# Turning the row maxima of four attention heads with one transpose of eight columns in a two-layer kernel

## The chip, the cores and the metric

The kernel runs on one NeuronCore of one Trainium2 chip. The metric is the time of one execution on the device in microseconds (us), less is better. Five engines work side by side, each through its own list of instructions in a fixed order: TensorE (PE in the profile, with its weight loads as PEld), VectorE (DVE), ScalarE (ACT), GpSimd (POOL) and SyncE (SP), which here only issues the DMAs. They wait for one another through semaphores.

## The reference, cut to what matters

Input is `x` of 8 sequences x 256 positions x 128 features in float32. There are two layers. The part that the change touches is the attention of layer 0, of which there are two kinds:

```python
# kind B: a cell of six nodes, each an attention with 8 heads of 16 features
scores = einsum('bqhd,bkhd->bhqk', qh, kh) / sqrt(16)
attn   = softmax(scores)                      # over the 256 keys
ctx    = einsum('bhqk,bkhd->bqhd', attn, vh)
# kind A: an encoder block with 16 heads of 8 features
att = softmax(einsum('nqd,nkd->nqk', qm, km)) # plus a relative position bias
```

A softmax needs, for every query of every head, the largest score of the row, which is subtracted before the exponential. Layer 1 is a state space block (convolution, scan, gating, a feed-forward part) and a mixture of eight experts; its work fills the engines beside the attention.

## The kernel before, in words

One sequence after the other is computed, with the next sequence's layer 0 overlapping the present one's layer 1. The work is cut into stages such as `("max", "B", g)` or `("expert", 3)`, in four lanes: the cell (kind B), its side work, the encoder block (kind A) and layer 1. For every engine the tables `PLACES` and `START` give each stage a place in time; `order(engine)` sorts by it, and that is the order in which the engine goes through its stages. Nothing is reordered at run time, so a stage that waits holds all that stands behind it on its engine. The change touches none of these tables.

Heads go in groups of four, each head's features in a strip of 32 partitions. A sequence has 12 groups of kind B and 4 of kind A, so 16 groups, and the program has 128. A group goes through these steps:

- `maximum` (TensorE, L785): 16 matrix products give the scores of four heads with the queries on the partitions, 4 heads x 2 halves of 128 queries x 256 keys, in two wide PSUM tiles, `strips`.
- `tops` (VectorE, L1307): two reductions over the keys leave `rowmax`, 128 partitions x (4 heads x 2 query halves), so one column per head and half.
- `max_rows` on TensorE (L793): `rowmax` is turned, so that the maxima lie along the free dimension. Two transposes are made, one for each query half: each has four columns as the stationary operand (one per head, every second column of `rowmax`) and the 128 x 128 identity as the moving operand, and writes 4 partitions x 128 of a PSUM bank.
- `max_rows` on ScalarE (L1059): a copy of 4 x 256 values from PSUM to `maxrow` in SBUF.
- `max_rows` on SyncE (L601): a DMA of 4 KB puts the four rows as one more row into each head's strip of the query tile. The key tile has -1 there.
- `score` (TensorE, L802): waits for that DMA (`maxed`), then computes the scores again, now with the keys on the partitions and the maximum already subtracted.
- `exp` (ScalarE, L1066), and `values` (TensorE, L815 and L822) follow.

Small products share three PSUM banks in turn. `take` (L694) waits until the stage that had the bank three uses ago has been read; the rows of maxima are one such use, and ScalarE's copy sets its bank free. `maxrow` has two buffers for each side and kind, which a copy may overwrite after the DMA of two groups before has landed.

Of the kernel before, what the change touches and what calls it, by code (L numbers as in the profile page):

```python
# [12 lines left out]
ACT = mybir.ActivationFunctionType  # L13
AX = mybir.AxisListType.X

P = 128
NSEQ, L, D = 8, 256, 128
# [6 lines left out]
STRIP = 32  # L24
# [155 lines left out]
def hybrid_layers(nc, t):  # L180

    ctx = ExitStack()
    with ctx:
        def sb(name, shape, dt=F32):
            return ctx.enter_context(nc.sbuf_tensor(name, shape, dt))

        def one(name):
            return ctx.enter_context(nc.semaphore(name))

        def sig(name, per, step=1, sides=1):  # L190
            return Signal([one(f"{name}{i}" if sides > 1 else name) for i in range(sides)], per, step)

        def past(eng, s, b, k=0):
            if b >= 0:
                eng.wait_ge(*s.at(b, k))
# [6 lines left out]
        ident = sb("ident", [P, P])  # L202
# [4 lines left out]
        rows = sb("rows", [P, t["rows"].shape[0], D])  # L207
# [44 lines left out]

        sides = {"B": 2, "A": 1}
        rowmax = {k: sb(f"rowmax_{k}", [P, n, 2, 4, 2]) for k, n in sides.items()}
        maxrow = {k: [[sb(f"maxrow_{k}{j}{i}", [4, L]) for i in range(2)] for j in range(n)] for k, n in sides.items()}
        probs = sb("probs", [P, 2, 4, 2, L])
        out_sb = sb("out_sb", [P, 2, 512])
        rsum_b = sb("rsum_b", [P, 2, BH])
# [113 lines left out]
        maxrow_done = {"B": sig("maxrow_done_B", 2 * NODES, 1, 2), "A": sig("maxrow_done_A", A_GROUPS)}  # L372
# [65 lines left out]
        s_strips, s_valued, s_ps = one("strips_ready"), one("valued"), one("ps_ready")  # L438
# [51 lines left out]
        def ready(eng, b, name):  # L490
            eng.wait_ge(s_ps, PS_AT[b, name] + 1)
# [12 lines left out]
        def bank(b, name):  # L504
            return BANK[b, name]
# [12 lines left out]
        def _(sp):  # L518
# [20 lines left out]
            for i in range(2):  # L539
                dst = bass.AP(tensor=a_scr.tensor, offset=i * AH * STRIP * L, ap=[[L, P], [P * L, A_GROUPS], [1, L]])  # L540
# [55 lines left out]
            def max_rows(b, kind, k):  # L596
                sp.wait_ge(*maxrow_done[kind].at(b, k))
                side, row = (b % 2, BW) if kind == "B" else (0, AW)
                x = qs["B"][side][:, k % 2, :] if kind == "B" else qs["A"][:, k, :]
                dst = bass.AP(tensor=x.tensor, offset=x.offset + row * x.ap[0][0], ap=[[STRIP * x.ap[0][0], 4], [1, L]])  # L600
                sp.dma_start(dst, maxrow[kind][side][k % 2][:, :]).then_inc(maxed[kind][k % 2].of(b), 16)  # L601

            def o_write(b):
# [19 lines left out]
            def store(b):  # L623
                sp.wait_ge(*acc_done.at(b, EX))
                hold(sp, s_held)
                sp.dma_start(t["out"][b].rearrange("(a p) d -> p a d", p=P), acc[:, :, :]).then_inc(out_stored.of(b), 16)

            run_stages("sync", {"load": load, "a_write": a_write, "rows": max_rows, "t_rows": t_rows, "a_stack": a_stack, "pos": positions, "v_read": v_read_,
                                "o_write": o_write, "o_read": o_read_, "weights": weights, "store": store})
            sp.wait_ge(*out_stored.at(NSEQ - 1))  # L630
# [3 lines left out]
        def _(pe):  # L634
# [3 lines left out]
            n = 0  # L638
# [11 lines left out]
            for c in range(NODES):  # L650
                (eq, _), (ek, _), (ev, _) = PLAN[c]
                o = setup_banks[n % len(setup_banks)]
                setup([(o[:, 0:2 * P], raw_we_t[:, eq, :], raw_wq[:, c, :, :], True, True),
                       (o[:, 2 * P:4 * P], raw_we_t[:, ek, :], raw_wk[:, c, :, :], True, True)], len(setup_banks))
                o = setup_banks[n % len(setup_banks)]
# [8 lines left out]
            for c in range(NODES - 1):  # L664
                pe.wait_ge(s_dve0, 2 * NODES)
                o = ps[n % 2]
# [27 lines left out]
            def take(b, name):  # L694

                if FREED[b, name]:
                    user, freed, k = FREED[b, name]
                    pe.wait_ge(*freed.at(user, k))
                return bank(b, name)
# [88 lines left out]
            def max_rows(b, kind, k):  # L788
                pe.wait_ge(*top_done[kind].at(b, 2 * k + 1))
                o = take(b, ("rows", kind, k))  # L790
                side = b % 2 if kind == "B" else 0
                for qc in range(2):
                    mm = pe.transpose(o[0:4, qc * P:(qc + 1) * P], rowmax[kind][:, side, k % 2, :, qc], ident[:, :])  # L793
                mm.then_inc(s_ps, 1)

            def score(b, kind, g):
                pe.wait_ge(*maxed[kind][g % 2].at(b, g // 2))
# [169 lines left out]
            def expert(b, i):  # L967
# [5 lines left out]
                for j in range(2):  # L973
# [7 lines left out]
            run_stages("tensor",  # L981
                       {"prep_t": prep_t, "aproj": aproj, "q": queries, "k": keys, "v": values_in,
                        "values_a": values_a, "max": maximum, "rows": max_rows, "score": score, "values": values,
                        "post_b": lambda b, c: post(b, "B", c), "post_a": lambda b, g: post(b, "A", g),
                        "ctx": ctx_t, "node": node, "gather": gather, "wo_y": wo_y, "ab_t": ab_t_, "ff_y": ff_y,
# [5 lines left out]
        def _(act):  # L991
# [59 lines left out]
            def max_rows(b, kind, k):  # L1051
                ready(act, b, ("rows", kind, k))
                n, sides_n = (2 * NODES, 2) if kind == "B" else (A_GROUPS, 1)

                if k >= 2:
                    act.wait_ge(*maxed[kind][k % 2].at(b, k // 2 - 1))
                else:
                    past(act, maxed[kind][k % 2], b - sides_n, n // 2 - 1)
                act.activation(maxrow[kind][b % sides_n][k % 2][:, :], bank(b, ("rows", kind, k))[0:4, 0:L], ACT.Copy).then_inc(maxrow_done[kind].of(b), 1)  # L1059

            def exp(b, kind, g, i):
                strips_ready(act, b, "score", kind, g)
# [125 lines left out]
            def expert(b, i):  # L1188
                ready(act, b, ("h", i))
                if i >= 2:  # L1190
# [3 lines left out]
            run_stages("scalar",  # L1194
                       {"prep_t": prep_t, "aproj": aproj, "q": queries, "k": keys, "v": values_in, "values_a": values_a,
                        "rows": max_rows, "exp": exp, "out": out, "ctx": ctx_t, "node": node, "gather": gather, "ab_t": ab_t_,
                        "z_t": z_t, "inproj": inproj, "xc": xc_tanh, "bcdt": bcdt, "sp_u": sp_u_, "sp_z": sp_z, "state": state,
                        "h_t": h_t_, "ffn": ffn, "ffn_t": ffn_t, "router": router, "expert": expert})
# [541 lines left out]
```

## Time and profile before

| | |
|---|---|
| Median of three runs | 1611.76 us (1611.71 to 1615.91) |
| The profiled execution's own time | 1618.7 us |
| Its span, first to last instruction | 1616.9 us |
| TensorE busy | 1284.9 us, 79% of the span |
| VectorE busy | 1067.4 us, 66% |
| ScalarE busy | 743.6 us, 46% |
| GpSimd busy | 272.7 us, 17% |
| Mean granted clock of TensorE | 0.905 of 2.4 GHz |

The profile is one execution on the chip. The granted clock is what part of full speed TensorE was given; 1.00 is 2.4 GHz and 0.50 is 1.2 GHz. The chain of waits is followed back from the last instruction: at each step to the work that released it, or to the instruction before it on its engine; "issue" on it is time in which the engine waited for nothing that the profile shows. The duration of one matrix product goes from its start to its modelled end, and products overlap, so what a product costs in a stream of others is the distance to the next start, and not its duration.

### The profile page before, as it was taken

The page shows a single profiled execution, that of the slowest core. Times are in us where ns is not written, and L with a number is a line of the kernel's source. Part 1 is how long each engine was busy: PE and PEld are TensorE (multiplying, and loading weights), DVE is VectorE, ACT ScalarE, POOL GpSimd, SP SyncE. Part 2 cuts the span into 40 slices and gives each one's busy share as a digit, 9 for nine tenths or more (in the row PEclk, how much of TensorE's full clock was granted, in tenths as well). Part 3 has the DMA queues.
Part 4 walks back from the last instruction along what each step waited for, and adds up shares of the span by engine and source line. Part 5 has one row for each costly group of instructions (what it writes and reads, how often), then busy time and mean ns, then how long its engine had stood idle before and what let it go on. Part 6 is the DMA issues. An engine that isn't in the chain of part 4 may idle for free.

```text
span 1616.9 us, 28690 instructions
## 1 busy us (share of the span) xinstructions
PE 1284.9 (79%) x10896; PEld 888.4 (55%) x10896; DVE 1067.4 (66%) x1757; ACT 743.6 (46%) x1420; POOL 272.7 (17%) x277
## 2 busy tenths in 40 slices
PE   6767787778997799878987899779987898678328
PEld 5434454445784468545764577446754675347217
DVE  2322335486768866896779676886689667857775
ACT  0133344455555554555545555555455554443322
POOL 0000002022101311131103210221013110321260
PEclk9777998889998999899998999899989998789659
DMA  5042020001210122002100211012200210012102
GB/s 200 7 72 23 2 44 8 1 6 46 54 55 3 25 63 70 5 14 70 49 29 14 54 46 49 2 25 64 70 5 17 68 57 18 14 29 71 42 1 69
DMA packets 108359, 62.98 MB, mean 39 GB/s; under 512 B 71169, under 2 KB 90145, under 8 KB 108097
## 3 DMA queue, kind: packets, MB, share of 16 engines
q1 hardware_dynamic: 108224, 61.15, 14.0%
q8 instruction: 90, 1.47, 0.4%
q14 instruction: 45, 0.36, 0.1%
HBM read 54.02 MB, written 6.59 MB: 37 GB/s over the span
## 4 chain that ended last, share of the span: by engine, by line
PE 56%; DVE 22%; issue 10%; ACT 9%; DMA 2%; POOL 1%; SPq 0%; DVEq 0%; ACTq 0%; POOLq 0%
PE strips L802 10%; PE strips L785 7%; PE ps L963 6%; PE ps L975 6%; PE attn_out L815 6%; DVE rowmax_B L1307 5%; ACT probs L1066 5%; DVE hb L1448 5%; DVE hb L1443 3%; PE ps L742 2%; PE attn_out L822 2%; DVE rowmax_A L1307 2%; PE ps L646 2%; DVE work L1417 2%; PE ps L793 1%
## 5 line engine op out<-in xcount | busy, mean ns | idle before, releaser
L1066 ACT ACTIVATE probs<-strips 128x1024 f32<-128x1024 f32 x256 | 248.9, 1021 | 133.0 <-PE strips L802 132.3
L1307 DVE TENSOR_REDUCE rowmax_B<-strips 128x4 f32<-128x1024 f32 x192 | 227.1, 1218 | 119.6 <-PE strips L785 119.5
L802 PE MATMUL strips<-qs_b,ks_b 32*128 32x256 f32 x1536 | 129.6, 457 | 75.3 <-ACT probs L1066 45.8
L1448 DVE TENSOR_TENSOR_SCAN hb<-da,hb 128x1024 f32<-128x1024 f32 x64 | 150.2, 2346 | 2.2
L1534 DVE SCALAR_TENSOR_TENSOR work<-hb,ps 128x512 f32<-128x512 f32 x128 | 86.5, 686 | 96.7 <-ACT hb L1192 96.2
L802 PEld LDWEIGHTS strips<-qs_b,ks_b 32*128 32x128 f32 x1536 | 83.3, 213 | 106.4 <-issue 103.4
L785 PE MATMUL strips<-ks_b,qs_b 32*128 32x256 f32 x1536 | 114.2, 412 | 23.1 <-ACT probs L1066 12.4
L975 PE MATMUL ps<-ze,w_e 128*128 128x256 f32 x512 | 127.3, 386 | 3.2 <-DVE work L1534 1.8
L963 PE MATMUL ps<-w_e,work 128*128 128x128 f32 x1024 | 125.1, 277 | 1.2 <-DVE work L1534 1.2
L963 PEld LDWEIGHTS ps<-w_e,work 128*128 128x128 f32 x1024 | 121.2, 192 | 8.1 <-DVE work L1534 4.5
L815 PE MATMUL attn_out<-probs,vb 128*32 128x256 f32 x1536 | 111.9, 419 | 9.2 <-ACT probs L1066 9.2
L1153 ACT ACTIVATE da<-gate,a_neg 128x255 f32<-128x255 f32 x256 | 108.0, 496 | 21.0 <-DVE hb L1448 16.9
L1192 ACT ACTIVATE hb<-ps 128x512 f32<-128x512 f32 x128 | 75.5, 597 | 88.5 <-PE ps L975 86.4
L1619 POOL TENSOR_TENSOR cv_t<-hb 128x512 f32<-128x512 f32 x56 | 71.1, 1270 | 245.1 <-DVE hb L1452 245.1
L785 PEld LDWEIGHTS strips<-ks_b,qs_b 32*128 32x128 f32 x1536 | 72.3, 189 | 58.3 <-issue 36.4
L975 PEld LDWEIGHTS ps<-ze,w_e 128*128 128x128 f32 x512 | 91.7, 190 | 22.6 <-issue 8.3
L1074 ACT ACTIVATE out_sb<-attn_out 128x512 f32<-128x512 f32 x80 | 47.8, 597 | 121.3 <-PE attn_out L822 73.7
L918 PE MATMUL ps<-bc,sel 96*128 96x256 bf16 x256 | 51.2, 319 | 55.1 <-DVE hb L1452 21.4
L1443 DVE TENSOR_TENSOR hb<-ps,dtx 128x1024 f32<-128x1024 f32 x64 | 77.9, 1217 | 24.3 <-PE ps L918 13.2
L1307 DVE TENSOR_REDUCE rowmax_A<-strips 128x4 f32<-128x1024 f32 x64 | 75.9, 1219 | 12.9 <-PE strips L785 12.9
L1621 POOL TENSOR_TENSOR cv<-cv,cv_t 128x512 f32<-128x512 f32 x56 | 82.3, 1470 | 4.4
L1452 DVE TENSOR_TENSOR hb<-hb,ps 128x1024 f32<-128x1024 f32 x64 | 78.1, 1221 | 2.2
(260 smaller groups left out, 2112.8 us busy)
## 6 DMA issues: line engine op xcount, KB each, us to landing
w_e<-in_w_e SPq DMA_DIRECT2D x128, 256.0 KB, 3.1
qs_a<-a_scr SPq DMA_DIRECT2D x8, 512.0 KB, 3.8
ks_a<-a_scr SPq DMA_DIRECT2D x8, 512.0 KB, 4.9
pos<-t_scr SPq DMA_DIRECT2D x8, 264.0 KB, 11.8
a_scr<-qkv_a SPq DMA_DIRECT2D x16, 128.0 KB, 4.1
qs_b<-maxrow_B SPq DMA_DIRECT2D x96, 4.0 KB
probs<-in_b_we_t SPq DMA_DIRECT2D x1, 1280.0 KB, 6.9
x_in<-in_x SPq DMA_DIRECT2D x8, 128.0 KB, 2.7
```

Source lines behind the costliest of these rows:

```text
L785: mm = pe.matmul(o, strip(qs, b, kind, g, j, qc * P, P), strip(ks, b, kind, g, j, 0, L), start=True, stop=True)
L802: mm = pe.matmul(o, strip(ks, b, kind, g, j, kc * P, P), strip(qs, b, kind, g, j, 0, L), start=True, stop=True)
L815: mm = pe.matmul(attn_out[32 * j:32 * j + 32, i * L:(i + 1) * L], v, heads[:, j, kc, :], start=(kc == 0), stop=(kc == 1))
L963: mm = pe.matmul(o[:, h * D:(h + 1) * D], eh[:, e % 2, j, h * P:(h + 1) * P], w_e2[:, (b * EX + e) % RING, j, :], start=(j == 0), stop=(j ...
L975: mm = pe.matmul(o[:, j * L:(j + 1) * L], w_e1[:, n % RING, f * P:(f + 1) * P], ze[:, :], start=True, stop=True)
L1066: act.activation(probs[:, group % 2, 2 * i:2 * i + 2, :, :].rearrange("p h a b -> p (h a b)"), strips[i][:, :], ACT.Exp).then_inc(s_exp, 1)
L1153: last = act.activation(da[:, k % 2, m, j, 1:L], dt[:, m, 1:L], ACT.Exp, scale=a_neg[:, m, 2 * k + j:2 * k + j + 1])
L1307: dve.tensor_reduce(out=rowmax[kind][:, b % sides_n, k % 2, 2 * i:2 * i + 2, :], in_=strips[i][:, :].rearrange("p (h q t) -> p h q t", h=2 ...
L1443: dve.tensor_tensor(hk, o, dtx[:, :, :].unsqueeze(2).to_broadcast([P, CH, 2, L]), ALU.mult).then_inc(hb_done.of(b), 1)
L1448: dve.tensor_tensor_scan(flat_h, flat_a, flat_h, 0.0, ALU.mult, ALU.add).then_inc(scan_done.of(b), 1)
L1534: dve.scalar_tensor_tensor(out=eh[:, e % 2, 2 * k:2 * k + 2, :], in0=eh_t[:, i % 2, :, :], scalar=1.0, in1=parts_of(bank(b, ("h", i)), 2), ...
L1621: pool.tensor_tensor(ysum[:, :, :], ysum[:, :, :], pair[:, :, :], ALU.add).then_inc(ysum_done.of(b), 1)
```

## The change

The two transposes of four columns become one transpose of all eight columns, into 8 partitions x 128. The eight columns are in the order (head, half), so that the output's partitions are too. The copy on ScalarE becomes 8 x 128 values instead of 4 x 256, the buffers `maxrow` take 8 partitions x 128 instead of 4 x 256, and the DMA reads 8 partitions of 512 bytes each and writes them into four rows of 1024 bytes as before, so the bytes are the same and its pieces are half as long. The order of the stages, the semaphores and their counts stay.

```diff
-        maxrow = {... sb(f"maxrow_{k}{j}{i}", [4, L]) ...}
+        maxrow = {... sb(f"maxrow_{k}{j}{i}", [8, P]) ...}
...
-                dst = bass.AP(tensor=x.tensor, offset=..., ap=[[STRIP * x.ap[0][0], 4], [1, L]])
+                dst = bass.AP(tensor=x.tensor, offset=..., ap=[[STRIP * x.ap[0][0], 4], [P, 2], [1, P]])
                 sp.dma_start(dst, maxrow[kind][side][k % 2][:, :]).then_inc(maxed[kind][k % 2].of(b), 16)
...
-                for qc in range(2):
-                    mm = pe.transpose(o[0:4, qc * P:(qc + 1) * P], rowmax[kind][:, side, k % 2, :, qc], ident[:, :])
-                mm.then_inc(s_ps, 1)
+                pe.transpose(o[0:8, 0:P], rowmax[kind][:, side, k % 2, :, :].rearrange("p h q -> p (h q)"), ident[:, :]).then_inc(s_ps, 1)
...
-                act.activation(maxrow[...][:, :], bank(b, ("rows", kind, k))[0:4, 0:L], ACT.Copy).then_inc(maxrow_done[kind].of(b), 1)
+                act.activation(maxrow[...][:, :], bank(b, ("rows", kind, k))[0:8, 0:P], ACT.Copy).then_inc(maxrow_done[kind].of(b), 1)
```

(`L` is 256 and `P` is 128.)

## Rows read from the trace of the kernel before

**Rows 1.** The page: the span, and the busiest engine.

```profile
span 1616.9 us, 28690 instructions
...
PE 1284.9 (79%) x10896; PEld 888.4 (55%) x10896; DVE 1067.4 (66%) x1757; ACT 743.6 (46%) x1420; POOL 272.7 (17%) x277
```

**Rows 2.** The page: the chain that ended last, by engine and by line.

```profile
PE 56%; DVE 22%; issue 10%; ACT 9%; DMA 2%; POOL 1%; SPq 0%; DVEq 0%; ACTq 0%; POOLq 0%
PE strips L802 10%; PE strips L785 7%; PE ps L963 6%; PE ps L975 6%; PE attn_out L815 6%; DVE rowmax_B L1307 5%; ACT probs L1066 5%; DVE hb L1448 5%; DVE hb L1443 3%; PE ps L742 2%; PE attn_out L822 2%; DVE rowmax_A L1307 2%; PE ps L646 2%; DVE work L1417 2%; PE ps L793 1%
```

**Rows 3.** Windows: stretch, busy us (instructions) per engine, TensorE clock, DMA share, GB/s.

```profile
497.20:500.70 3.50, 3.50 (x22) 2.50 (x19) 3.36 (x5) 1.77 (x2) 0.00 (x0) 0.51 0.02 5
541.60:671.30 129.70, 116.18 (x1077) 84.43 (x1077) 89.79 (x175) 68.16 (x127) 19.55 (x23) 1.00 0.17 46
671.30:674.70 3.40, 3.39 (x21) 2.41 (x22) 3.23 (x6) 1.25 (x2) 0.00 (x0) 0.50 0.02 5
671.30:715.70 44.40, 33.47 (x266) 19.95 (x266) 40.34 (x36) 23.84 (x51) 12.68 (x10) 0.81 0.04 13
```

**Rows 4.** The chain in order of time (start us, us, what), places with L793.

```profile
82.65 0.59 PE ps L793 x2
...
751.87 0.38 PE ps L793 x2
752.25 1.07 PE strips L785 x16
...
794.29 0.87 PE ps L975 x4
795.16 0.22 PE ps L793 x2
795.38 1.07 PE strips L785 x16
...
849.49 0.36 ACT maxrow_A L1059
```

**Rows 5.** Line 793: durations ns min/median/max with first and last start; below, who waited for it.

```profile
L793 PEld LDWEIGHTS ps<-ident,rowmax_B x192: 82/85/130, 78.7 to 1451.2; 128*4 128x4 f32 x192
L793 PE MATMUL ps<-ident,rowmax_B x192: 269/273/421, 78.7 to 1451.4; 128*4 128x128 f32 x192
...
  ACT maxrow_B L1059: 76.4, 31
```

**Rows 6.** Groups by line: columns as on the page; ScalarE's copy and neighbours, then a weight load.

```profile
L1059 ACT ACTIVATE maxrow_B<-ps 4x256 f32<-4x256 f32 x96 | 34.2, 362 | 76.4 <-PE ps L793 76.4
L1074 ACT ACTIVATE out_sb<-attn_out 128x512 f32<-128x512 f32 x80 | 47.8, 597 | 121.3 <-PE attn_out L822 73.7 <-PE attn_out L815 47.6
L995 ACT ACTIVATE a_neg<-a_neg 128x32 f32<-128x32 f32 x1 | 0.2, 213 | 0.0
L815 PEld LDWEIGHTS attn_out<-probs,vb 128*32 128x32 f32 x1536 | 44.4, 118 | 61.6 <-issue 30.1 <-ACT probs L1066 16.5
```

**Rows 7.** Timeline of one group of kind A, 738 to 742 us.

```profile
738.23 0.38 PE L793 MATMUL ps<-ident,rowmax_A 128*4 128x128 f32 x2
738.65 0.37 ACT L1059 ACTIVATE maxrow_A<-ps 4x256 f32<-4x256 f32 x1
739.05 0.50 SPq L601 DMA_DIRECT2D qs_a<-maxrow_A  x1
741.56 0.53 PEld L802 LDWEIGHTS strips<-qs_a,ks_a 32*128 32x128 f32 x12
```

**Rows 8.** Timeline of the same group of the first sequence, 221 to 224 us.

```profile
221.88 0.53 SPq L601 DMA_DIRECT2D qs_a<-maxrow_A  x1
...
223.56 0.53 PEld L802 LDWEIGHTS strips<-qs_a,ks_a 32*128 32x128 f32 x12 [0.60 <-DMA qs_a<-maxrow_A]
```

**Rows 9.** DMA issues: count, KB each, median us from issue to landing.

```profile
v_scr<-qkv_a SPq DMA_DIRECT2D x8, 128.0 KB, 3.5
...
a_scr<-qs_a SPq DMA_DIRECT2D x1, 16.0 KB, 1.4
```

More of the change, by code:

```diff
@@ L254, in hybrid_layers @@
         rowmax = {k: sb(f"rowmax_{k}", [P, n, 2, 4, 2]) for k, n in sides.items()}
-        maxrow = {k: [[sb(f"maxrow_{k}{j}{i}", [4, L]) for i in range(2)] for j in range(n)] for k, n in sides.items()}
+        maxrow = {k: [[sb(f"maxrow_{k}{j}{i}", [8, P]) for i in range(2)] for j in range(n)] for k, n in sides.items()}
         probs = sb("probs", [P, 2, 4, 2, L])
@@ L599, in max_rows @@
                 x = qs["B"][side][:, k % 2, :] if kind == "B" else qs["A"][:, k, :]
-                dst = bass.AP(tensor=x.tensor, offset=x.offset + row * x.ap[0][0], ap=[[STRIP * x.ap[0][0], 4], [1, L]])
+                dst = bass.AP(tensor=x.tensor, offset=x.offset + row * x.ap[0][0], ap=[[STRIP * x.ap[0][0], 4], [P, 2], [1, P]])
                 sp.dma_start(dst, maxrow[kind][side][k % 2][:, :]).then_inc(maxed[kind][k % 2].of(b), 16)
@@ L1058, in max_rows @@
                     past(act, maxed[kind][k % 2], b - sides_n, n // 2 - 1)
-                act.activation(maxrow[kind][b % sides_n][k % 2][:, :], bank(b, ("rows", kind, k))[0:4, 0:L], ACT.Copy).then_inc(maxrow_done[kind].of(b), 1)
+                act.activation(maxrow[kind][b % sides_n][k % 2][:, :], bank(b, ("rows", kind, k))[0:8, 0:P], ACT.Copy).then_inc(maxrow_done[kind].of(b), 1)
             def exp(b, kind, g, i):
```

## The prediction, made before the changed kernel was built or run

> **What bounds the kernel now.** I read the page first. TensorE is the fullest engine, busy 1284.9 us of a span of 1616.9 us, with VectorE at 66% [rows 1]. That is a mean, so I looked at the chain of waits next: TensorE holds 56% of it, VectorE 22%, ScalarE 9%, and the line of the change, L793, about 1% [rows 2]. So there is something to win on the path itself, but no more than that percent.
>
> Then the time by stage. The program repeats itself: the clock falls at 497.2 us and again at 671.3 us, 174.1 us later, one sequence [rows 3]. In the 129.7 us after 541.6 us TensorE is busy for 116.18 us at full clock (1.00, the 2.4 GHz level), and in the 44.4 us after 671.3 us for 33.47 us with VectorE at 40.34 us and the clock at 0.81 on average, with whole stretches at the 1.2 GHz level (0.50) [rows 3]. The long part is bound by TensorE, the short one by VectorE.
>
> Last, the places where the pair of transposes stands on the chain [rows 4]. I followed the chain through the whole span and counted 65 of the 128 pairs on it, wholly or in part: 14 in the first 275 us, then 8 of the 16 pairs of each of the six sequences in the middle, 3 at the end. The rows show the three forms: 0.38 us where the chain comes from a wait (751.87 us), 0.22 us where TensorE runs without a gap (795.16 us), 0.59 us at the low clock (82.65 us).
>
> **The change part by part.**
>
> *One transpose fewer, 128 times.* Two in a gapless stream take 0.22 us [rows 4], so one takes 0.11 us. The same comes out of a pair that starts after a wait: one lasts 0.27 us [rows 5], two 0.38 us [rows 4]. At the low clock the second starts some 0.17 to 0.21 us after the first (an estimate: the longest single one is 0.421 us [rows 5], the pair 0.59 us [rows 4]). All 128 together are 128 x 0.11 = 14 us at least. What lies on the path: 65 pairs, of which 5 are at the low clock, so 60 x 0.11 + 5 x 0.2 = 7.6 us; I take **7.5 us**, some pairs being on the chain in part. The other 63 pairs stand where TensorE waits for something else soon after, and I cost them at nothing: their cover is that wait, and if it goes too, they bring up to 63 x 0.11 = 7 us more.
>
> *Eight columns of weights for four.* Four take 82 ns [rows 5], 32 columns take 118 ns [rows 6]. By the straight line between them eight take 87 ns. The load lies beside the matrix product before it (0.11 us in a stream), so I cost it at nothing. If it stood free it would be 65 x 0.005 = 0.3 us, which also is the bound.
>
> *The copy on ScalarE.* 256 columns take 0.362 us, 512 take 0.597 us, so a column is 0.92 ns and 128 columns should take 0.24 us; the bounds are 0.213 us, the shortest copy-like row with 32 columns, and 0.362 us, no gain [rows 6]. This makes ScalarE 128 x 0.12 = 15 us less busy. On the chain the copy appears twice, once at 849.49 us [rows 4] and once in the first sequence, where the landing of the maxima ends the wait of `score` [rows 8]. So it brings **0.2 us**. The PSUM bank also comes free some 0.2 us earlier; nobody is seen waiting for it, and I cost that at nothing.
>
> *The DMA.* The bytes are the same in pieces of 512 bytes for 1024. SyncE's issue takes 0.5 us [rows 7], and SyncE has nothing urgent behind it, so even twice that would be hidden. From issue to use, where the use waited for it, it is 1.68 us [rows 8]; where it did not, 2.51 us [rows 7]. So in the closest stage that recurs for each sequence the data lies ready 0.83 us before its use. The change has no row here. A DMA of 16 rows and 16 KB lands in 1.4 us [rows 9], so twice the pieces should cost 0.1 us at most, less than the 0.22 us by which the DMA will be issued earlier. The far bound is the scattered 128 KB DMA, 3.5 us [rows 9]. I take no change, being nearest to the small one.
>
> The Trainium skill bears on this (DMA: Bandwidth & Descriptors, "Why a DMA increments its semaphore by 16 and not by 1"): a DMA is spread over as many engines as divide the slowest dimension of both sides. By that, four heads on one side keep it on four engines, as before, and each gets two pieces for one; the eight source partitions bring no spreading. No row here shows it, and the sum would be the same.
>
> **The sum.** 7.5 + 0.2 = 7.7 us off the profiled execution's own 1618.7 us (span 1616.9 us), giving 1611.0 us. The median of the runs is 1611.76 us, 6.9 us below the profiled one, and the saving is the same number of transposes there: 1611.76 - 7.7 = **1604.0 us**, 0.48% less. A measurement of this kernel can tell about 0.3%, 4.8 us, from no change.
>
> **The rivals.**
>
> *The gain is given back to the clock: 1611.5 us.* Each sequence loses TensorE time in the stretches at 1.2 GHz, and the sequences repeat at the distance at which these stretches do, 174.1 us [rows 3]. If TensorE's work comes 0.87 us earlier per sequence (8 x 0.109), other products fall into a slow stretch. A slow stretch of 3.4 us full of products [rows 3] costs up to 1.7 us against the high clock, so half a stretch more per sequence pays back all of it. For it speaks that TensorE is full at 497 and 671 us while slow; against it, that the shift can as well bring the work out of the slow stretch. The other way to the same number: a VectorE or ScalarE branch right behind the chain. The eight places stand between TensorE's own products, so I hold that to be small.
>
> *More than the chain: 1598.5 us.* Some of the 63 other pairs and the 15 us of ScalarE count too, or the clock shift falls well, for 5 us beyond the sum.
>
> *The page's smaller transpose: 1608.2 us.* If a second transpose, following on the first, took half of what the rows say, 0.055 us, the path would win 65 x 0.055 = 3.6 us. The row with two in 0.22 us speaks against it [rows 4]. The Trainium skill (TensorE: Matmul & The Clock Gate, "Wait — 56ns, not 53.3ns?") states 55.6 ns from start to start for 128 columns at 2.4 GHz; that was measured with bf16, here the data is float32, and the trace does not agree.
>
> *Slower, the DMA lands late: 1622 us.* The place is the wait of `score` (L802) for `maxed`. The landing may be later by 0.83 + 0.22 = 1.05 us before even the closest stage feels it. At the far bound of 3.5 us for 1.68 us it is 1.82 us later, which stalls that stage for 0.77 us per sequence; an estimate of three such stages of the 16 makes 3 x 0.77 x 8 = 18.5 us, less 7.7 us. It decides from about 1.4 us later on, where the stalls (3 x 0.35 x 8 = 8.4 us) pass the gain. Against it stands the 1.4 us of the 16-row DMA.
>
> *Slower by the clock: 1618 us.* The same shift with a whole slow stretch more per sequence, 8 x 1.7 us = 13.6 us less 7.7 us.
>
> **How the numbers follow.** The forecast has 0.52, the gain given back 0.25, more than the chain 0.09, the page's transpose 0.03, the late DMA 0.05, the clock's slower case 0.06. The predicted time is the forecast's. Around it, the clock moves things by some 3 us either way, so nearly all of the forecast lies below 1606.9 us (0.3%). Faster by over 0.3%: 0.52 + 0.09, less 0.01 for its upper edge, 0.60. Within 0.3%: 0.25 + 0.03 + 0.02 (that edge, and the smallest slower cases), 0.30. Slower: 0.10. The range reaches from the better case, 1598 us, to the case given back with its own spread, 1615 us; what lies out is the two slower cases and the far end of the better one.
>
> **What the profile of the changed kernel should show.** L793 with 128 products of 128x8 for 256, mean still about 0.27 us; on the chain "L793 x1" with 0.11 us in a stream and 0.27 us after a wait. L1059 with 8x128 at 0.24 us. The use behind the DMA of the first sequence 1.7 us after its issue. Distances between equal events of two sequences of about 173.3 us for 174.1 us. The forecast is wrong if that distance stays at 174.1 us while the transposes are halved (clock, or another branch), or if L802 is seen waiting for the maxima more often than in the first sequence.

## The result, and the profile of the changed kernel

The changed kernel takes 1617.55 us (median of 22 runs), the kernel before 1612.76 us (22 runs beside them): a ratio of 1.0027, 95% interval 1.0016 to 1.0039. Forecast were 1604.0 us, and the measured time lies above the range of 1598 to 1615 us. The mean granted clock of the changed kernel's 22 runs is 0.899 (0.894 to 0.906). For the kernel before, 35 runs that were taken beside the experiments have 0.909 (0.904 to 0.916).

The page of the changed kernel (span, busy engines, the clock in 40 slices, the chain by line), against [rows 1, 2]:

```profile
span 1618.7 us, 28434 instructions
...
PE 1275.8 (79%) x10768; PEld 883.9 (55%) x10768; DVE 1068.2 (66%) x1757; ACT 730.0 (45%) x1420; POOL 272.6 (17%) x277
...
PEclk9778997788998899989998999879998999799659
...
PE 56%; DVE 22%; issue 10%; ACT 9%; DMA 1%; POOL 1%; SPq 0%; DVEq 0%; ACTq 0%; POOLq 0%
```

TensorE has 128 instructions and 9.1 us less to do, ScalarE 13.6 us less, and the span is no shorter. The lines of the change, which are now 792 and 1057, answer to [rows 5] and [rows 6]; `score` is now line 800:

```profile
L792 PEld LDWEIGHTS ps<-ident,rowmax_B x96: 82/86/132, 77.8 to 1452.6; 128*8 128x8 f32 x96
L792 PE MATMUL ps<-ident,rowmax_B x96: 269/273/421, 77.8 to 1452.8; 128*8 128x128 f32 x96
```

```profile
L1057 ACT ACTIVATE maxrow_B<-ps 8x128 f32<-8x128 f32 x96 | 23.9, 254 | 71.8 <-PE ps L792 71.8
```

The parts are all as small as forecast: the transpose lasts 273 ns as each of the two did, its weight load 86 ns for 85, the copy 254 ns for 362. The chain in order of time (start us, us, what), against [rows 4], has the single transpose with 0.27 us after a wait and 0.11 us in a stream:

```profile
755.11 0.27 PE ps L792
...
798.29 0.11 PE ps L792
798.40 1.08 PE strips L785 x16
```

The same eight places per sequence stand on it, and a ninth with one transpose at the low clock (0.31 us, at 676.28, 850.52, 1024.80 and 1201.62 us). The DMA is no later either. In the first sequence, where its landing ends the wait, the timeline has issue and use 1.65 us apart, for 1.68 us in [rows 8]:

```profile
222.36 0.54 SPq L601 DMA_DIRECT2D qs_a<-maxrow_A  x1
224.01 0.74 PEld L800 LDWEIGHTS strips<-qs_a,ks_a 32*128 32x128 f32 x16 [0.45 <-DMA qs_a<-maxrow_A]
```

So the time went elsewhere. The clock tells where, at the place of the second long fall in a sequence, and it does so in two forms. First the form that is easier to see. Windows of the kernel before (columns as in [rows 3]: stretch, busy us and instructions of PE, PEld, DVE, ACT, POOL, then clock, DMA share, GB/s), around that fall:

```profile
708.90:715.70 6.80, 4.89 (x28) 3.07 (x28) 6.73 (x6) 3.42 (x9) 2.53 (x2) 0.50 0.24 81
715.70:719.10 3.40, 2.17 (x37) 1.36 (x40) 2.50 (x3) 3.35 (x8) 1.51 (x2) 1.00 0.00 0
719.10:722.50 3.40, 3.40 (x40) 1.45 (x32) 2.63 (x3) 0.60 (x1) 1.06 (x1) 1.00 0.01 2
```

And the same place of the changed kernel:

```profile
710.30:717.10 6.80, 4.96 (x39) 3.26 (x32) 6.73 (x6) 3.59 (x10) 2.53 (x2) 0.50 0.23 78
717.10:720.50 3.40, 1.56 (x24) 0.86 (x18) 2.88 (x2) 3.06 (x6) 0.41 (x1) 1.00 0.00 0
720.50:723.90 3.40, 3.40 (x36) 1.35 (x32) 2.35 (x2) 0.76 (x4) 2.13 (x2) 0.50 0.03 7
```

Both come back from 1.2 to 2.4 GHz. In the stretch that follows, the kernel before is busy for 2.17 us, the changed one for 1.56 us; and then the clock stays up in the one and falls again in the other, for 3.4 us that are full of products (3.40 of 3.40). TensorE's timelines of that place. The kernel before:

```profile
714.89 0.98 PE L793 MATMUL ps<-ident,rowmax_B 128*4 128x128 f32 x4
717.10 1.15 PE L785 MATMUL strips<-ks_b,qs_b 32*128 32x256 f32 x16 [1.23 <-ACT probs L1066]
718.17 1.07 PE L815 MATMUL attn_out<-probs,va 128*32 128x256 f32 x16
```

The changed kernel:

```profile
717.30 0.38 PE L792 MATMUL ps<-ident,rowmax_B 128*8 128x128 f32 x2
719.52 1.19 PE L785 MATMUL strips<-ks_b,qs_b 32*128 32x256 f32 x16 [1.83 <-ACT probs L1064]
720.64 1.94 PE L813 MATMUL attn_out<-probs,va 128*32 128x256 f32 x16
```

Groups 9 and 0 of kind B (the latter of the next sequence) are turned here back to back: four transposes, 0.98 us and mostly at 1.2 GHz, became two, 0.38 us at 2.4 GHz, and the wait for ScalarE's exponentials behind them grew by these 0.6 us, from 1.23 to 1.83 us. The 16 products of L813, which took 1.07 us, then run at half the clock for 1.94 us.

This second fall is not where most of the time is lost, though. Sequence by sequence, from the first scan of one to that of the next, the kernel before has

```profile
503.45:677.76 174.31, 149.65 (x1342) 104.38 (x1342) 130.23 (x209) 91.88 (x177) 32.23 (x33) 0.95 0.14 38
```

and the changed kernel

```profile
505.06:680.97 175.91, 150.72 (x1328) 104.92 (x1328) 130.14 (x209) 90.72 (x179) 32.19 (x33) 0.92 0.14 37
680.97:855.18 174.21, 146.91 (x1328) 103.01 (x1326) 130.80 (x210) 90.42 (x178) 32.20 (x33) 0.95 0.14 38
855.18:1029.36 174.18, 147.01 (x1327) 103.18 (x1326) 130.71 (x209) 90.34 (x178) 32.21 (x33) 0.95 0.14 38
1029.36:1206.31 176.95, 151.48 (x1328) 104.98 (x1328) 130.03 (x210) 90.57 (x178) 32.20 (x33) 0.91 0.14 37
```

The two in the middle have the second fall and are as long as before, at the same clock of 0.95. The first and the last have 0.92 and 0.91 and are 1.6 and 2.6 us longer. There the clock does not come back at this place at all. The same place in the first of these sequences, by windows and then by TensorE's timeline, in the kernel before:

```profile
534.80:541.60 6.80, 4.98 (x28) 3.06 (x28) 6.73 (x6) 3.42 (x9) 2.54 (x2) 0.50 0.25 81
541.60:545.00 3.40, 2.21 (x37) 1.45 (x40) 2.49 (x3) 3.25 (x8) 1.61 (x2) 1.00 0.00 0
```

```profile
540.69 1.01 PE L793 MATMUL ps<-ident,rowmax_B 128*4 128x128 f32 x4
542.90 1.15 PE L785 MATMUL strips<-ks_b,qs_b 32*128 32x256 f32 x16 [1.20 <-ACT probs L1066]
543.97 1.07 PE L815 MATMUL attn_out<-probs,va 128*32 128x256 f32 x16
...
547.26 1.15 PE L802 MATMUL strips<-qs_b,ks_b 32*128 32x256 f32 x16
```

In the changed kernel:

```profile
536.20:543.00 6.80, 4.66 (x26) 2.81 (x26) 6.73 (x6) 3.09 (x8) 2.53 (x2) 0.50 0.23 78
543.00:549.85 6.85, 5.45 (x48) 2.65 (x48) 4.05 (x4) 3.13 (x8) 2.53 (x2) 0.50 0.02 4
```

```profile
542.19 0.59 PE L792 MATMUL ps<-ident,rowmax_B 128*8 128x128 f32 x2
544.40 2.09 PE L785 MATMUL strips<-ks_b,qs_b 32*128 32x256 f32 x16 [1.62 <-ACT probs L1064]
546.41 1.94 PE L813 MATMUL attn_out<-probs,va 128*32 128x256 f32 x16
...
550.52 1.15 PE L800 MATMUL strips<-qs_b,ks_b 32*128 32x256 f32 x16
```

The work stands alike against the slow stretch in both: L785 starts 8.1 us after the stretch's start before (542.90 and 534.80) and 8.2 us after it now (544.40 and 536.20). TensorE is busy for 4.98 us of the stretch's first 6.80 us in the one and for 4.66 us in the other. Then the kernel before has its clock back, and the changed one stays at 1.2 GHz for 6.85 us more. From L785 to the next scores it takes 6.12 us for 4.36, so 1.76 us are lost here. With the second fall it is 5.23 us (719.52 to 724.75), so 0.86 us, which does not show in the length of the sequence.

### The profile page after: what moved, and what is told of

The parts are those of the page before. It is cut to its first block, busy times and chain, and to the rows that moved or that the text cites. A ratio compares the mean times of both kernels' runs of the same rounds, so it can differ in the third digit from the quotient of the medians.

```text
span 1618.7 us, 28434 instructions
## 1 busy us (share of the span) xinstructions
PE 1275.8 (79%) x10768; PEld 883.9 (55%) x10768; DVE 1068.2 (66%) x1757; ACT 730.0 (45%) x1420; POOL 272.6 (17%) x277
## 4 chain that ended last, share of the span: by engine, by line
PE 56%; DVE 22%; issue 10%; ACT 9%; DMA 1%; POOL 1%; SPq 0%; DVEq 0%; ACTq 0%; POOLq 0%
PE strips L800 9%; PE strips L785 7%; PE ps L961 6%; PE ps L973 6%; DVE hb L1446 6%; PE attn_out L813 6%; DVE rowmax_B L1305 5%; ACT probs L1064 5%; DVE hb L1441 3%; PE ps L742 2%; PE attn_out L820 2%; DVE rowmax_A L1305 2%; PE ps L646 2%; DVE work L1415 2%; PE ps L848 1%
## 5 line engine op out<-in xcount | busy, mean ns | idle before, releaser
L800 PE MATMUL strips<-qs_b,ks_b 32*128 32x256 f32 x1536 | 126.3, 447 | 78.4 <-ACT probs L1064 46.6
L785 PE MATMUL strips<-ks_b,qs_b 32*128 32x256 f32 x1536 | 119.9, 429 | 26.8 <-ACT probs L1064 16.1
L813 PE MATMUL attn_out<-probs,vb 128*32 128x256 f32 x1536 | 109.6, 412 | 8.8 <-ACT probs L1064 8.8
L785 PEld LDWEIGHTS strips<-ks_b,qs_b 32*128 32x128 f32 x1536 | 75.7, 196 | 59.8 <-issue 36.4
```

The costliest lines, as they stand in the source:

```text
L785: mm = pe.matmul(o, strip(qs, b, kind, g, j, qc * P, P), strip(ks, b, kind, g, j, 0, L), start=True, stop=True)
L800: mm = pe.matmul(o, strip(ks, b, kind, g, j, kc * P, P), strip(qs, b, kind, g, j, 0, L), start=True, stop=True)
L813: mm = pe.matmul(attn_out[32 * j:32 * j + 32, i * L:(i + 1) * L], v, heads[:, j, kc, :], start=(kc == 0), stop=(kc == 1))
```

## The experiments

Theory A was that the clock falls, or stays down, for want of these products; B, that the copy or the half pieces of the DMA cost the time; C, that only the shift of the work against the clock's stretches counts. Theory D came up after the first runs: that a sequence stays about 174.1 us long whatever is taken off TensorE's path. Times are medians, ratios are to the kernel before in the same session; the clock is the mean over a kernel's timed runs.

**Filling the groups again.** In the changed kernel, ahead of the real transpose and into columns that nobody reads:

```diff
+                if <condition>:
+                    pe.transpose(o[0:8, P:2 * P], rowmax[kind][:, side, k % 2, :, :].rearrange("p h q -> p (h q)"), ident[:, :])
                 pe.transpose(o[0:8, 0:P], ...).then_inc(s_ps, 1)
```

The condition is "always" in e1, the eight groups off the chain in e2, the eight on it in e3, B 0 and B 9 in e4, and all but these two in e13.

> The changed kernel with a second transpose of the same eight columns (into unused columns of the bank, ahead of the real one) in all 16 groups of a sequence: TensorE is as full as before, the copy of 8x128 and the DMA of half pieces are the changed kernel's. Theory A (the clock: fewer products leave TensorE at 1.2 GHz for longer): the time of the kernel before, 1610 to 1614 us, mean clock 0.903 to 0.907. Theory B (the copy or the DMA of half pieces cost the time): 1617 us or more, clock as in the changed kernel. Theory C (what counts is only how early the work comes against the clock's stretches): 1610 to 1614 us as well.

> The second transpose only in the eight groups of a sequence whose pair was not on the chain (kind B 0, 1, 2, 7, 8, 9, kind A 1, 2), so TensorE has its old load there and the eight places on the chain stay 0.11 us shorter. Theory A: the clock of the kernel before (0.903 to 0.907) and the gain on the path, 1603 to 1608 us. Theory B: 1617 us. Theory C (shift alone, load off the chain is of no account): as the changed kernel, 1616 to 1619 us, clock 0.898.

> The reverse: the second transpose in the eight groups that were on the chain (kind B 3, 4, 5, 6, 10, 11, kind A 0, 3), one transpose in the others. Theory A: the low clock of the changed kernel (about 0.898) without its gain, 1619 to 1625 us. Theory B: 1617 us. Theory C (the shift is undone): the time of the kernel before, 1610 to 1614 us, clock 0.904.

> The second transpose only in groups 0 and 9 of kind B, which stand together at 715 us of the kernel before, just where its clock came back to 2.4 GHz. Theory A in its narrow form (the load at this one place decides when the clock comes back): nearly as with all eight, 1603 to 1609 us, clock 0.903 or more. Theory A in its wide form (load anywhere in the VectorE-bound part): between, 1608 to 1616 us. Theories B and C: as the changed kernel, 1616 to 1619 us.

> The counterpart of e4: the second transpose in 14 of the 16 groups, all but B 0 and B 9. Theory A, narrow (the two transposes taken away at this place are what holds the clock down longer): the clock of the changed kernel, 0.897 to 0.902, and 1616 to 1622 us, though 14 of the 16 groups are as full as before. Theory A, wide: 1612 to 1615 us, clock 0.907 or more.

| kernel | transposes per sequence | median us | ratio (95%) | mean clock |
|---|---|---|---|---|
| before | 32 | 1614.74 | | 0.909 |
| changed | 16 | 1617.55 | 1.0027 (1.0016 to 1.0039) | 0.899 |
| e1, all filled | 32 | 1613.17 | 0.9997 (0.9983 to 1.0012) | 0.910 |
| e2, off the chain | 24 | 1614.20 | 1.0008 (0.9991 to 1.0025) | 0.905 |
| e3, on the chain | 24 | 1616.97 | 1.0015 (1.0001 to 1.0029) | 0.900 |
| e4, B 0 and B 9 alone | 18 | 1613.08 | 0.9993 (0.9978 to 1.0008) | 0.906 |
| e13, all but B 0 and B 9 | 30 | 1621.77 | 1.0043 (1.0027 to 1.0059) | 0.900 |

(The 1614.74 us are those of the session of e1 to e4; the changed kernel's ratio is to the 1612.76 us of its own session.) Theory B falls with e1, which has the changed kernel's copy and DMA and the time of the kernel before. e4 and e13 settle the place: two transposes given back, at B 0 and B 9, bring back the clock and the time, and 14 given back everywhere else do not. e1 and e13 differ in these two alone, and are 8.6 us apart. The window of e4 behind its slow stretch is as busy as that of the kernel before, and the clock stays up:

```profile
705.40:708.90 3.50, 3.27 (x22) 1.65 (x20) 3.47 (x3) 2.29 (x5) 0.73 (x1) 0.51 0.13 51
708.90:712.30 3.40, 2.21 (x36) 1.45 (x40) 2.50 (x3) 2.92 (x8) 1.72 (x2) 1.00 0.02 5
712.30:715.70 3.40, 3.40 (x37) 1.56 (x30) 2.57 (x4) 0.60 (x2) 0.84 (x1) 1.00 0.01 2
```

That of e13 has the 1.56 us of the changed kernel, and the second fall behind it:

```profile
708.00:714.80 6.80, 5.24 (x40) 3.55 (x36) 6.73 (x6) 3.83 (x11) 2.54 (x2) 0.50 0.24 81
714.80:718.20 3.40, 1.56 (x26) 0.86 (x18) 3.00 (x2) 3.00 (x5) 0.28 (x1) 1.00 0.00 0
718.20:721.60 3.40, 3.40 (x39) 1.38 (x32) 2.36 (x2) 0.82 (x4) 2.25 (x2) 0.50 0.01 2
```

The traces agree over the five sequences in the middle of each. In the kernel before, e1, e2 and e4, which all have the second transposes at B 0 and B 9, the clock is back 0.9 to 1.5 us before this L785 in 20 of 20 places and does not fall again there. In the changed kernel, e3 and e13, which lack them, this happens in none of 15: the slow stretch goes on in two, three and three of the five, and the others have the second fall. The two forms cost e13 as they cost the changed kernel: 177.3 us for sequences of the first (501.49 to 678.80 us), 174.3 us for the second (678.80 to 853.12 us). Why a sequence takes the one form or the other was not tested.

What missed: e2 was to be at 1603 to 1608 us and e4 at 1603 to 1609 us, with the shorter path as a gain on top, and both are only level with e1 and the kernel before. That raised theory D. e2 fills B 0 and B 9 as well and is no better than e4. e3 was to be at 1619 us or more and is at 1616.97 us, level with the changed kernel although its path is as long as that of the kernel before; e13, with six more transposes than e3, all off the chain, is 4.8 us slower than it. Neither is explained.

**Holding the clock up.** Useless transposes of eight columns of the identity, while TensorE waits anyway. They write to `attn_out`, and a wait that is added with them makes sure that its last contents have been copied by then, so that these kernels have more waits as well as more products:

```diff
+            def busy(*stage):
+                at = last_group[0]
+                if stage in FILL and at is not None:
+                    pe.wait_ge(s_out, at + 1)
+                    for _ in range(FILL[stage]):
+                        pe.transpose(attn_out[0:8, 0:P], ident[:, 0:8], ident[:, :])
```

> The changed kernel with useless transposes of eight columns of the identity in the waits of TensorE that the trace shows ahead of the falls of the clock: 20 ahead of the scores of B 6 (wait 3.9 us), 10 ahead of state step 1 (1.8), 16 ahead of the rows of A 2 (2.9), 10 ahead of the values of cell step 4 (2.1), 6 ahead of the maxima of B 1 (1.2); 62 per sequence, their results unused. Theory A (the clock falls for want of products): clock 0.94 or more, and at the slope over all runs (0.93 us for each 0.001 of the clock) 1575 to 1600 us. Theory C (only the shift counts): no gain; up to 1625 us if the added work reaches the path.

> The kernel before with the same 62 added transposes per sequence. Theory A: the clock as in e5 and, since the clock no longer answers to the change, the whole gain of the path apart from it, so 5 to 8 us slower than e5. If instead the change is slower by itself (theory B), e5 is slower than this one.

> The changed kernel with the added transposes only around the second fall of the clock (rows of A 2, values of cell step 4, maxima of B 1; 32 per sequence). Theory A: the fall at 710 us of the changed kernel goes and the one at 673 us stays; clock 0.92 or more, 1590 to 1608 us. Theory C: 1612 to 1620 us.

> The changed kernel with the added transposes only around the first fall (scores of B 6, state step 1; 30 per sequence). Theory A: the fall at 673 us goes and the one at 710 us stays; clock 0.91 or more, 1595 to 1611 us. Theory C: 1612 to 1620 us.

> The changed kernel with more of the added transposes, 107 per sequence for 62: 32 ahead of the scores of B 6, 14 at state step 1, 24 at the rows of A 2, 18 at the values of cell step 4, 9 at the maxima of B 1, 10 at the scores of B 8. Theory A (the clock falls for want of products): clock 0.94 or more and 1585 to 1603 us, unless the added work now outlasts the waits (then up to 1612 us at a high clock).

> The kernel before with the same 107 added transposes per sequence. Theory A: with the clock up in both, the change is worth its path, so 5 to 8 us slower than e9. Theory D (the length of a sequence is pinned near 174.1 us, whatever is taken off TensorE's path): within 3 us of e9.

> e5 (the changed kernel with 62 added transposes per sequence in the waits) and, with it, the second transpose in B 0 and B 9. Narrow theory A: clock at least that of e5 (0.933), 1600 to 1605 us. If the clock at this place is held by the other added products already: as e5, 1603 to 1607 us.

> e14 with 74 added transposes per sequence for 62 (24, 12, 20, 12, 6). Theory A: clock 0.935 to 0.94 and 1599 to 1606 us; if the added products outlast the waits as in e9, 1607 to 1615 us.

| kernel | added per sequence | median us | ratio (95%) | mean clock |
|---|---|---|---|---|
| e5, changed | 62 | 1605.16 | 0.9944 (0.9923 to 0.9965) | 0.933 |
| e6, before | 62 | 1607.27 | 0.9963 (0.9945 to 0.9981) | 0.937 |
| e7, changed | 32, second fall | 1612.38 | 0.9993 (0.9979 to 1.0006) | 0.916 |
| e8, changed | 30, first fall | 1625.68 | 1.0070 (1.0050 to 1.0090) | 0.903 |
| e9, changed | 107 | 1618.37 | 1.0021 (1.0004 to 1.0038) | 0.939 |
| e10, before | 107 | 1622.96 | 1.0053 (1.0036 to 1.0070) | 0.940 |
| e14, changed | 62, and B 0, B 9 | 1602.31 | 0.9928 (0.9915 to 0.9942) | 0.936 |
| e16, changed | 74, and B 0, B 9 | 1602.74 | 0.9934 (0.9921 to 0.9948) | 0.938 |

Work that computes nothing makes the kernel faster: e5 by 0.56%, e14 by 0.72% against the kernel before. In e14 the place that is at 0.50 in the kernels without added work is at 1.00 in this sequence (two of the five in the middle keep a slow stretch of 3.4 us there, at 1049.9 and 1224.0 us):

```profile
700.00:705.00 5.00, 3.00 (x34) 2.24 (x34) 4.97 (x5) 2.85 (x8) 2.53 (x2) 1.00 0.31 107
705.00:710.00 5.00, 4.05 (x58) 2.39 (x54) 4.93 (x4) 3.95 (x8) 0.95 (x1) 1.00 0.00 0
```

The page of e14 has a span of 1599.3 us. There is a limit: with 107 added the clock is no higher and the time is lost again, though why is not separated (the added products may outlast some waits, or the clock may do so elsewhere). The expectations of e5 were on the optimistic side (1575 to 1600 us): the slope from run to run of one kernel, 0.93 us for each 0.001 of mean clock (a least-squares line common to the 105 runs of the kernel before, the changed one and e1 to e4), does not carry over to a clock held up by added work. e8 was a plain miss. Filling the first fall alone gave 12.7 us more than the kernel before, for the expected 1595 to 1611 us. The first fall did not go, and the second grew:

```profile
532.00:545.60 13.60, 10.06 (x71) 5.94 (x75) 11.66 (x9) 7.81 (x19) 5.06 (x4) 0.50 0.13 41
```

This is the long stretch over B 9 and B 0 again, here in all five sequences in the middle, which last 175.4 to 176.1 us. Why filling the first fall brings it about has no tested cause. Other misses: e7 was to reach a clock of 0.92 and 1590 to 1608 us, and the second fall only became shorter; e9 was to stay below 1612 us; e6 was to be 5 to 8 us slower than e5 and is 2.1 us slower, at the higher clock (0.937 for 0.933).

e9 and e10 are the cleanest price of the change itself, since their mean clocks are alike (0.939 and 0.940): 1622.96 - 1618.37 = 4.6 us faster, for the 7.7 us of the sum. The runs without added work agree: the two changed runs with a clock of 0.905 and 0.906 took 1612.3 us each, and the six runs of the kernel before at 0.905, over all sessions, took 1614.5 to 1619.6 us.

**Shortening and lengthening the path by other means.** All in the kernel before. e11 leaves out three quarters of the sum in the second product of one of the eight experts, e12 in three of them, so their outputs are not those of the reference; they serve as a shorter path only:

```diff
             def expert_y(b, e):
...
-                    for j in range(FF):
-                        mm = pe.matmul(..., start=(j == 0), stop=(j == FF - 1))
+                    parts = 1 if e in (4,) else FF        # e12: (2, 3, 4)
+                    for j in range(parts):
+                        mm = pe.matmul(..., start=(j == 0), stop=(j == parts - 1))
```

e15 adds two transposes in each of the eight groups on the chain, in the manner of e1.

> The kernel before, in which the second product of one expert of eight (expert 4) adds up one quarter of its inner dimension instead of four: 12 of 16 products fall away, by the page's 1.78 us for 16 some 1.3 us per sequence on TensorE's path at the full clock, 10.7 us in all. It stands for any shortening of the path. Theory A alone (the clock answers to the load in the VectorE-bound part, which is untouched): 1601 to 1606 us, sequences of 172.8 us. Theory D (pinned): the gain shows up in less than a third, 1609 to 1615 us, sequences of 174.0 to 174.1 us.

> The same with three experts (2, 3, 4), 4.0 us per sequence, 32 us in all. Theory A alone: 1580 to 1585 us, sequences of 170.1 us. Theory D: either still pinned (1600 us or more) or let go to a shorter length, 1585 to 1595 us, with sequences at equal distances of about 170.7 us.

> The kernel before with two more transposes in each of the eight groups on the chain, which makes the path 8 x 2 x 0.11 = 1.75 us per sequence longer, 14 us in all, and leaves the other groups alone. Theory A alone: 1626 to 1629 us. Theory D (lengths pinned at 174.1 us from both sides): 1613 to 1619 us. If it is a bound from below alone, the full 14 us: sequences of 175.9 us.

| kernel | path per sequence | median us | ratio (95%) | mean clock |
|---|---|---|---|---|
| e11 | 1.3 us shorter | 1612.46 | 0.9992 (0.9979 to 1.0004) | 0.906 |
| e12 | up to 4.0 us shorter | 1602.03 | 0.9925 (0.9905 to 0.9944) | 0.906 |
| e15 | 1.75 us longer | 1622.25 | 1.0050 (1.0031 to 1.0069) | 0.913 |

From 10.7 us less work e11 gains 0.9 us, from up to 32 us e12 gains 11.3 us; e15 pays 8.4 of its 14 us. The windows over three sequences, from the first scan of one to that of the third after it, first the kernel before:

```profile
503.45:1025.53 522.08, 448.76 (x4027) 312.84 (x4028) 391.20 (x627) 276.32 (x532) 96.67 (x99) 0.95 0.14 38
```

e4, whose path is up to 0.87 us per sequence shorter:

```profile
496.55:1018.72 522.17, 444.44 (x3986) 311.42 (x3984) 390.40 (x627) 271.43 (x532) 96.62 (x99) 0.95 0.14 38
```

e11, where three times 1.3 us are missing:

```profile
498.99:1020.68 521.69, 445.25 (x3992) 309.45 (x3992) 390.66 (x627) 277.40 (x533) 96.81 (x99) 0.95 0.14 38
```

522.08, 522.17 and 521.69 us: 174.0 us per sequence in all three, though TensorE does 4 us less in the latter two. e12 went down to 172.2 us per sequence (516.46 for three) and e15 up to 175.7 us (527.06). In e4 the five sequences in the middle last 174.04 to 174.13 us, its slow stretches stand 174.1 us apart as well, and L785 at B 0 starts 1.24 to 1.26 us after the clock's return in each. So theory D holds in a weak form. Around the kernel before, a shorter path brings a lower mean clock (e1 0.910, e4 0.906; before 0.909, e11 0.906) and next to no time, while a longer path costs 60% of its length. Part of e12's 4 us was not on the path either: new waits of 0.6 and 0.5 us stand in TensorE's timeline among the experts' products (at 619 and 630 us), and its sequences alternate between 173.0 and 171.7 us. By what mechanism the gain is taken back, in three profiles to within 0.2 us per sequence, stays open; that work and clock keep step in e4 fits a length that settles on the distance of the slow stretches, but no run tests it. The span of a single profile says nothing on this: that of e4 is 6.5 us shorter than that of the kernel before (1610.4 for 1616.9 us), and 6.4 us of it lie before the first scan (322.51 for 328.94 us).

## Why the prediction was wrong

*Which parts were right.* The costs: 0.11 us for the transpose in a stream, the weight load (87 ns forecast, 86 measured), the copy (0.24 us forecast, 0.254 us measured), the DMA (1.65 us from issue to use for 1.68). The eight places per sequence on the chain are the same and shrank as said. The rivals with a late DMA and with the page's smaller transpose are out. (The rival "more than the chain" is 5 us beyond the sum by its words, which is 1599.0 us and not 1598.5.)

*The step that failed* is the one on the other 63 pairs: "I cost them at nothing: their cover is that wait". For the time on the path that is so. But the pairs of B 0 and B 9 kept TensorE busy in a wait at the end of a slow stretch, just ahead of dense products. Without the second transposes the wait grew (1.62 us for 1.20), and the clock either stayed down over the dense part, 14 or 17 us for 7, or came back and went down once more. The first makes a sequence 176 to 177 us long for 174.2. e13, with only these two taken away, is slower than even the changed kernel, and e4, with only these two given back, is level with the kernel before. The rival "slower by the clock" (1618 us, chance 0.06) had the size, but in part by luck: its 1.7 us are what a long stretch costs at this place (1.76 us), and it has them in every sequence, where the trace of the changed kernel has them in two of five. It gave as its cause the shift of the work, and that is not what the runs show: e2 and e4 have the shorter path and keep the clock, and in the changed kernel the clock stays down where the work stands as before against the slow stretch (8.2 us for 8.1).

*The second step* is the sum's 7.5 us on the path. At a like clock 4.6 us of 7.7 are there (e9 against e10); at the clock that the kernels get by themselves, none is (e4 against e1: 1613.08 and 1613.17 us). The forecast named the sign of this, sequences that stay at 174.1 us while the transposes are halved (the changed kernel has 174.2 us, and 175.9 and 177.0 us in the long ones, for 173.3 forecast), but gave the rival behind it 0.25, and took the gain of a shorter path as passed on in full. That the median of three runs stood 6.9 us below the profiled one was a warning: over all its runs the kernel before spreads over 1606.6 to 1624.9 us with its clock (0.916 to 0.895), more than the change was to bring.

*The Trainium skill* (TensorE: Matmul & The Clock Gate, "Part 4: PE-mode transpose") says that transposes do not bring the clock up in the way that other products do. A reader who followed it would expect no harm from leaving some out. The runs do not agree: the products added in e5 are transposes alone, and the mean clock rose from 0.899 to 0.933; two transposes per sequence fewer took it from 0.910 (e1) to 0.900 (e13). (The page's figures there are for bf16, and these are float32.)

## What to carry to other kernels

Work on TensorE that lies in a wait is not free to remove: look at the granted clock in the windows around it, and at whether dense products follow. Look at several repeats and price the harm by the length of the whole sequence: the fall that was easiest to see here cost 0.86 us at its place and nothing in the length, and the stretch that went on cost 1.6 to 2.6 us. When an edit makes everything locally cheaper and the whole is not faster, compare the mean clock over many runs first, then put the removed load back at one place at a time, as e4 and e13 do. Once the place is known, a few useless products in TensorE's waits can be worth more than the edit: e14 is 0.72% faster than the kernel before, where the edit alone was 0.27% slower.

## What the runs showed of the hardware that was not expected

Two transposes, 0.2 us at the full clock, beside some 150 us of products per sequence, decide whether the clock comes back after 6.8 us or stays at half for 13.6 us and more. The time of one and the same kernel follows its mean clock closely from run to run, by 0.93 us for each 0.001. Added transposes lifted the mean clock from 0.899 to at most 0.94, and doing it at one of two places only (e8) made the kernel 0.7% slower. The length of a sequence stood at 174.0 us under three different loads. The issue of the DMA on SyncE went from 508 to 531 ns (medians, kind B) with the pieces halved, and from issue to use it is 1.65 us for 1.68.
